# One adaLN block (linear attention and a mixture of experts), with the operations of every engine in a new order

## What is computed

```python
mod = (silu(c) @ wmod).reshape(16, 6, 1, -1)
sa, ca, ga, sb, cb, gb = (mod[:, i] for i in range(6))
ga = (2 * (ga >= 0) - 1) * maximum(abs(ga), 0.25)      # gb likewise
h = layernorm(x) * (1 + ca) + sa
x = x + ga * attn(h)
h = layernorm(x) * (1 + cb) + sb
x = x + gb * ffn(h)

def attn(x):                                           # 16 heads of 8
    q, k, v = x @ Wq.T + bq, x @ Wk.T + bk, x @ Wv.T + bv
    q = softmax(q, over the 8 of a head); k = softmax(k, over tokens)
    out = q @ (k.T @ v)                                # per head
    return layernorm(out) * ln_g + ln_b, then @ Wo.T + bo

def ffn(x):                                            # 8 experts, top 2
    p = softmax(x @ router_w); top_p, top_e = top_k(p, 2)
    return sum over the 2 of top_p * (gelu(x @ w_in[e] + b_in[e]) @ w_out[e] + b_out[e])
```

## Time and profile before

| | |
|---|---|
| median of 3 runs | 365.6 us (364.08 to 366.45) |
| span of the profiled execution | 363.4 us |
| PE busy | 346.1 us (95%) |
| PE weight loads | 305.2 us (84%) |
| DVE busy | 302.1 us (83%) |
| ACT busy | 275.3 us (76%) |
| POOL busy | 224.8 us (62%) |
| chain that ended last | PE 67%, DVE 14%, issue 6%, DMA 5%, ACT 4% |

### The profile page before, as it was taken

How to read it: one execution, slowest core, us unless ns; L and a number is a source line. 1 busy time by engine, 2 the same in 40 slices (tenths; PEclk the granted TensorE clock), 3 DMA queues, 4 the chain that set the end, 5 groups by cost and what they waited for, 6 DMA issues and landing times.

```text
span 363.4 us, 9785 instructions
## 1 busy us (share of the span) xinstructions
PE 346.1 (95%) x3308; PEld 305.2 (84%) x3308; DVE 302.1 (83%) x1068; ACT 275.3 (76%) x500; POOL 224.8 (62%) x219
## 2 busy tenths in 40 slices
PE   8687899999999999989999999999999999999995
PEld 7365679898788989979898988989898989988885
DVE  3989999699799889979799897969998887864733
ACT  4465799877878888788797979797987968696740
POOL 3167454885826568683758758483866778382842
PEclk9878999999999999999999999999999999999999
DMA  7560055531325343170625343340807042244471
GB/s 217 139 236 0 3 178 203 175 120 62 147 87 177 115 164 132 37 249 9 203 92 175 118 170 124 97 169 4 289 3 262 3 150 87 76 190 119 177 262 58
DMA packets 19112, 47.94 MB, mean 132 GB/s; under 512 B 2603, under 2 KB 6390, under 8 KB 18806
## 3 DMA queue, kind: packets, MB, share of 16 engines
q1 hardware_dynamic: 18832, 47.16, 38.1%
q10 hardware_dynamic: 230, 0.15, 0.1%
HBM read 42.82 MB, written 4.48 MB: 130 GB/s over the span
## 4 chain that ended last, share of the span: by engine, by line
PE 67%; DVE 14%; issue 6%; DMA 5%; ACT 4%; POOL 2%; SPq 1%; DVEq 0%; ACTq 0%; POOLq 0%
PE pY L1113 24%; PE pH L1097 7%; PE pH L1098 6%; PE pH L1099 6%; PE pQV L1060 3%; DMA gate_bc<-route_scratch 3%; PE pC L1067 2%; PE pQV L1021 2%; DMA route_scratch<-gateT 2%; PE pC L1054 2%; PE pQV L1037 1%; PE pQV L1023 1%; PE pQV L1022 1%; PE pA L1000 1%; PE pB L1074 1%
## 5 line engine op out<-in xcount | busy, mean ns | idle before, releaser
L1113 PE MATMUL pY<-wout,v 128*128 128x128 f32 x1024 | 129.1, 275 | 0.9 <-DVE v L1630 0.9
L1113 PEld LDWEIGHTS pY<-wout,v 128*128 128x128 f32 x1024 | 124.6, 191 | 5.7 <-DVE v L1630 2.2
L441 POOL TENSOR_TENSOR v<-u,gate_bc 128x512 f32<-128x512 f32 x48 | 68.6, 1433 | 61.3 <-ACT u L769 47.9
L769 ACT ACTIVATE u<-pH,cols 128x512 f32<-128x512 f32 x128 | 85.4, 686 | 15.7 <-PE pH L1099 14.3
L1630 DVE TENSOR_TENSOR v<-u,gate_bc 128x512 f32<-128x512 f32 x80 | 68.0, 858 | 13.3 <-DMA gate_bc<-route_scratch 8.1
L1097 PE MATMUL pH<-h_hi,win_hi 128*128 128x512 f32 x128 | 59.0, 461 | 0.2
L1098 PE MATMUL pH<-h_hi,win_lo 128*128 128x512 f32 x128 | 50.5, 394 | 0.0
L1099 PE MATMUL pH<-h_lo,win_hi 128*128 128x512 f32 x128 | 50.4, 394 | 0.0
L717 ACT ACTIVATE xn<-x_all,nmr,rstd 128x128 f32<-128x128 f32 x64 | 26.3, 485 | 10.3 <-POOL nmr L460 10.2
L453 POOL TENSOR_TENSOR h_lo<-h,h_hi 128x512 fp32r<-128x512 f32 x15 | 20.6, 1370 | 16.1 <-ACT h_hi L697 16.1
L458 POOL TENSOR_TENSOR rstd<-ve,neg_half 128x4 f32<-128x4 f32 x16 | 18.6, 1159 | 18.9 <-DVE nm L1587 18.9
(11 more groups left out here) (169 smaller groups left out, 772.1 us busy)
## 6 DMA issues: line engine op xcount, KB each, us to landing
gate_bc<-route_scratch SPq DMA_DIRECT2D x64, 512.0 KB, 5.1
x_all<-in_L_attn_x SPq DMA_DIRECT2D x16, 256.0 KB, 3.2
out<-x_all SPq DMA_DIRECT2D x15, 256.0 KB, 2.2
gates<-gate_scratch SPq DMA_DIRECT2D x1, 1792.0 KB, 6.2
route_scratch<-gateT SPq DMA_DIRECT2D x64, 4.0 KB
gb_bc<-gb_scratch SPq DMA_DIRECT2D x1, 1024.0 KB, 4.6
win<-in_L_ffn_w_in SPq DMA_DIRECT2D x1, 512.0 KB, 4.3
wout<-in_L_ffn_w_out SPq DMA_DIRECT2D x1, 512.0 KB, 5.6
```

The costliest lines, as they stand in the source:

```text
L441: pool.tensor_tensor(v[:, e % U, :], u[:, e % U, :], gate_bc[:, b % 2, e, :], ALU.mult).then_inc(s["vp_done"], 1)
L769: act.activation(u[:, e % U, :], pH[:, e % 2, :], ACT.Gelu_apprx_tanh, bias=cols[:, e:e + 1]).then_inc(s["gelu_done"], 1)
L1113: i = mm(pY[:, t * P:(t + 1) * P], v[:, e % U, t * P:(t + 1) * P], wout[:, e, :], start=False, stop=(e == NE - 1), skip_group_check=True)
```

## The change

The `step` functions and their loops are gone: all five lists are written out for all 16 batches, in orders that differ from those before from the first calls to the last. The operations themselves are the same. Two helpers get a wait more: `ln1_stats(n)` waits for the aggregates of `ln1_var(n - 1)` and `ln2_stats(n)` for those of `ln2_var(n - 1)`. The diff is some 2,000 lines; this is its core, the beginnings of the lists and the two waits. In the part left out, the lists go on in the same manner to batch 15. At the end of POOL's list `residual2(14)` stands ahead of `weigh(15, 5)`, and the call of `residual2(15)`, which does nothing, is gone.

```diff
--- before.py
+++ after.py
@@ -294,68 +294,114 @@
...
+            load_x(1)
+            load_bias()
             load_experts()
-            load_bias()
-            load_x(1)
             load_x(2)
+            load_x(3)
+            load_x(4)
             store_mod_gates()
-            load_x(3)
+            spread_later_gates()
             spread_first_gates()
+            load_x(5)
             load_expert_bias()
-            spread_later_gates()
-            for b in range(-1, 8):
-                step(b)
+            store_gates(0)
+            spread_gates(0, 0)
+            store_moe_gates()
+            spread_moe_gates()
+            spread_gates(0, 1)
+            load_x(6)
+            spread_gates(0, 2)
+            spread_gates(0, 3)
+            store_gates(1)
+            spread_gates(1, 0)
+            spread_gates(1, 1)
+            load_x(7)
+            spread_gates(1, 2)
+            spread_gates(1, 3)
+            store_gates(2)
+            spread_gates(2, 0)
+            spread_gates(2, 1)
+            store_out(0)
+            spread_gates(2, 2)
+            spread_gates(2, 3)
...
@@ -459,196 +505,173 @@
...
+            masks()
             rstd_L(0)
-            masks()
             rstd_L(1)
+            h_low(1)
             gated_weight(0)
             gated_const(0)
+            gated_const(1)
             rstd_L(2)
-            h_low(1)
-            gated_const(1)
             gated_weight(1)
             rstd_O(0)
             expert_low()
-            rstd_L(3)
             h_low(2)
             rstd_B(0)
             h2_low(0)
+            rstd_L(3)
+            rstd_O(1)
+            rstd_L(4)
             gated_weight(2)
-            rstd_O(1)
-            gated_const(2)
-            h_low(3)
             gated_weight(3)
             rstd_B(1)
             weigh(0, 1)
+            h_low(3)
             weigh(0, 3)
+            weigh(0, 5)
+            gated_const(2)
+            gated_const(3)
+            h2_low(1)
             rstd_O(2)
-            rstd_L(4)
-            h2_low(1)
-            weigh(0, 5)
-            gated_const(3)
+            h_low(4)
...
             rstd_B(15)
+            residual2(12)
             weigh(14, 1)
             weigh(14, 3)
             h2_low(15)
@@ -656,10 +679,8 @@
             residual2(13)
             weigh(15, 1)
             weigh(15, 3)
+            residual2(14)
             weigh(15, 5)
-            residual2(14)
-            for b in range(15, 24):
-                step(b)
...
@@ -768,47 +789,25 @@
...
             ln1_apply(0)
+            h_evac_first()
             attention_weights()
-            h_evac_first()
             exp_k(0)
             ln1_apply(1)
             ek_evac(0)
+            h_evac(1)
             exp_q(0)
             expert_high()
-            h_evac(1)
+            qT_evac(0)
             sw_evac(0)
-            qT_evac(0)
             out_square(0)
+            exp_k(1)
             ln1_apply(2)
-            exp_k(1)
             ek_evac(1)
             h_evac(2)
             exp_q(1)
+            sw_evac(1)
             ln2_apply(0)
-            sw_evac(1)
             qT_evac(1)
             h2_evac(0)
             out_square(1)
@@ -817,114 +816,292 @@
             ln1_apply(3)
             gateT_evac(0)
             ek_evac(2)
-            h_evac(3)
             exp_q(2)
             gelu(0, 0)
+            gelu(0, 1)
+            h_evac(3)
+            gelu(0, 2)
+            gelu(0, 3)
             sw_evac(2)
-            gelu(0, 1)
-            gelu(0, 2)
             qT_evac(2)
-            gelu(0, 3)
+            ln1_apply(4)
+            out_square(2)
             ln2_apply(1)
-            out_square(2)
             gelu(0, 4)
+            gelu(0, 5)
+            gelu(0, 6)
             h2_evac(1)
+            exp_router(1)
             exp_k(3)
-            ln1_apply(4)
+            exp_q(3)
+            gelu(0, 7)
...
@@ -1113,264 +1290,477 @@
...
             modulation()
+            hT_first()
+            turn_rows()
             turn_weights()
-            turn_rows()
-            hT_first()
             residual_gates()
+            kT(0)
             keep_clock()
-            kT(0)
             qv(0)
+            ek_back(0)
             keep_clock()
-            ek_back(0)
+            hT(1)
+            keep_clock()
             gain_centred()
             keep_clock()
-            hT(1)
             state(0)
             keep_clock()
+            kT(1)
+            q_turn(0)
             state_weights(0)
-            keep_clock()
-            q_turn(0)
-            keep_clock()
             attend_centred(0)
-            kT(1)
+            attend_project(0)
             qv(1)
-            attend_project(0)
             ek_back(1)
             hT(2)
+            keep_clock()
             state(1)
+            state_weights(1)
             keep_clock()
             kT(2)
-            state_weights(1)
+            keep_clock()
             q_turn(1)
             h2T(0)
-            keep_clock()
             attend_centred(1)
             logits(0)
             qv(2)
+            hidden(0, 0)
+            ek_back(2)
             keep_clock()
-            ek_back(2)
+            gate_turn(0)
             attend_project(1)
-            gate_turn(0)
             hT(3)
-            hidden(0, 0)
+            state(2)
             hidden(0, 1)
-            state(2)
+            hidden(0, 2)
+            state_weights(2)
+            hidden(0, 3)
+            q_turn(2)
             moe_bias(0)
-            state_weights(2)
-            kT(3)
-            hidden(0, 2)
-            q_turn(2)
-            hidden(0, 3)
             hidden(0, 4)
+            hidden(0, 5)
             attend_centred(2)
             combine(0, 0)
-            h2T(1)
             combine(0, 1)
             qv(3)
-            hidden(0, 5)
+            h2T(1)
+            hidden(0, 6)
+            kT(3)
+            attend_project(2)
+            hidden(0, 7)
             logits(1)
-            attend_project(2)
-            ek_back(3)
-            hidden(0, 6)
             combine(0, 2)
-            hT(4)
             combine(0, 3)
             combine(0, 4)
+            hidden(1, 0)
+            ek_back(3)
             gate_turn(1)
+            hidden(1, 1)
+            hidden(1, 2)
+            combine(0, 5)
+            hT(4)
+            hidden(1, 3)
+            hidden(1, 4)
             state(3)
-            hidden(0, 7)
-            hidden(1, 0)
-            combine(0, 5)
-            hidden(1, 1)
+            combine(0, 6)
+            q_turn(3)
             state_weights(3)
-            combine(0, 6)
-            hidden(1, 2)
-            q_turn(3)
-            hidden(1, 3)
+            kT(4)
+            combine(0, 7)
...
+            attend_centred(6)
+            kT(7)
+            attend_project(6)
+            logits(5)
+            qv(7)
+            ek_back(7)
             hidden(4, 3)
-            h2T(5)
-            kT(7)
-            attend_centred(6)
             hidden(4, 4)
-            logits(5)
+            moe_bias(4)
+            combine(4, 0)
+            combine(4, 1)
+            gate_turn(5)
             hidden(4, 5)
-            qv(7)
-            attend_project(6)
-            moe_bias(4)
             hidden(4, 6)
...
@@ -1466,6 +1856,7 @@
 
             def ln1_stats(n):
                 dve.wait_ge(s[f"x{n % XS}_loaded"], DMA * (n // XS + 1))
+                w(dve, "mv1_done", T * n)
                 for t in range(T):
...
@@ -1574,6 +1965,7 @@
 
             def ln2_stats(n):
                 dve.wait_ge(s["x1_ready"], T * n + T)
+                w(dve, "mv2_done", T * n)
                 for t in range(T):
...
@@ -1650,283 +2042,417 @@
...
             ln1_stats(0)
+            ln1_var(0)
             silu_turned()
-            ln1_var(0)
             ln1_apply_first()
+            ln1_stats(1)
             modulation_columns()
+            h_evac_half()
             columns()
+            h_low_first()
             attention_low()
-            h_evac_half()
-            h_low_first()
+            ln1_var(1)
+            k_max(0)
             attention_gates()
-            k_max(0)
-            ln1_stats(1)
-            ln1_var(1)
+            centring()
             q_bias(0)
-            centring()
             q_max(0)
             q_shift(0)
+            gained_weight()
             v_bias(0)
-            gained_weight()
+            q_sum(0)
+            q_inv(0)
+            q_norm(0)
+            k_inv(0)
+            state_out(0)
+            k_max(1)
             ln1_stats(2)
-            q_sum(0)
-            k_inv(0)
-            q_inv(0)
-            state_out(0)
-            q_norm(0)
             ln1_var(2)
             expert_gates()
+            out_var(0)
             ln1_stats(3)
-            ln1_var(3)
-            out_var(0)
-            k_max(1)
             q_bias(1)
+            v_bias(1)
             q_max(1)
             residual1(0)
-            k_inv(1)
```

(55 more changed lines are left out.)

1280 lines of the change are left out of this document (878 added, 402 removed).

## The result

The change made the kernel 3 to 4% slower. The forecast was 367.6 us, half a per cent slower.

What follows compares the result with a forecast made beforehand. PE was taken as the bound after the fill, with DVE full from 18 to 54 us. Span 363.4 + 0.7 (start) + 1.3 (94 to 340) = 365.4, plus 2.2 to the median: 367.6 us, range 362.0 to 371.5.

Steps and rivals of the forecast that it cites:

- +0.7 us for the start: Lag of finished PE work left at 94 us after the fill; bounds -1.5 to +3.5 us.
- the gb row: Expert gates of batch 0: gb_bc ahead of the second quarter; DVE stands 2.5 us at weigh(0,2), about 0.9 at weigh(0,4).
- +1.3 us for 94 to 340: PE idle from 94 to 340 us: 3.3 us expected against 2.0 before.
- The gates of the first batch: Small broadcast queues behind the large one, gates land at 23.2 us; DVE's sum of squares 1.05 us late.
- the walk: New lists stepped through with trace durations: PE work 2.4 us behind at 60 us, 1.6 at 75, 0.7 at 94.
- Rival 2: Slower by the DMA order: both stalls go through, gaps at upper rate, 372.9 us (370.4 with only the first); chance 0.22.
- my rates: PE idle per us in written-out stretches: 0.0235 early, 0.0035 late, mean 0.0135; 0.9 to 5.8 us from 94 to 340.
- Does a new order make PE's work cheaper?: PE, whole run: 25 fewer switches to three-pass products cost and gain nothing; only idle time can move.
- PE busy changed by more than 1 us: Sign that the forecast is wrong: it would mean neighbours have a price; forecast was within 0.5 us of 346.1.
- the two waits at 0: Added waits in ln1_stats and ln2_stats on DVE: between 0 and 1.1 us over the run, taken as 0.
- the first 12 us: Start: some tenths saved, but first kT at 11.15 us for 10.89, a loss of 0.3 us; ga_rows at about 14.9.
- the drain: End of the last batch: residual2(14) goes ahead of weigh(15,5) while POOL waits anyway; 0 us.

Runs made afterwards that it cites:

- c2_a94: a3_both's orders for what has started by 94 us, the orders of the kernel before behind; 367.39 us, 1.0055 of before.
- a3_both: Changed kernel with the small first-gates broadcast ahead of the large one and the gb row's store and broadcast behind quarters 1 and 2; 370.14 us, 1.0169.
- b1_later: Kernel before with only the 1792 KB broadcast moved ahead of the 256 KB one; 369.51 us, 1.0128 of before.
- f2_again: The changed kernel once more, nothing edited, for a second profile; 380.64 us, 1.0415 of before.
- a1_first: Changed kernel with only the 256 KB broadcast of the first gates issued ahead of the 1792 KB one; 370.34 us, 1.0177 of before.
- c1_waits: Kernel before with its orders written out as lists and the two added waits; 365.25 us, 1.0013 of before.
- h3_both: The same kernel as a3_both, run in another launch on another chip; 370.40 us, 1.0150 of before.
- f1_six: a3_both with six calls on PE's list, where PE idled behind 160 us, moved behind one to three followers; 375.64 us, 1.0281 of before.
- i2_route: i1_mid's kernel with the router chain of batch 6 put back to before's places on all lists; 369.68 us, 1.0137 of before.
- h1_again: The changed kernel again, nothing edited, in a launch on another chip; 379.14 us, 1.0358 of before.
- i1_mid: Kernel before with the changed orders (a3_both's lists) only from 160 to 200 us; 369.78 us, 1.0155 of before.

## Why the prediction was wrong, step by step

Two terms of the sum failed. The +0.7 us for the start stood for 9.5 us by the runs: 6.3 (the first gates), 1.2 (the gb row) and 2.0 (the rest, c2_a94). The +1.3 us for 94 to 340 stood for some 5, and PE's own work, put at 0, was part of that.

**The first gates: the mechanism right, the size wrong three times.** The chain of "The gates of the first batch" came out link by link: `ga_rows` stored at 14.55 (I had it ready at 14.9), the large broadcast issued at 16.01 (16.37 by my sum), the small one behind it at 16.39. Then the first wrong term: from there the 6.2 + 0.6 us were 9.0. The gates were home at 25.0 and not 23.2. I had taken the large broadcast's landing from a trace that issues it at 20.36, not at 16; that it shares the DMA engines with more at 16 is likely, and no run isolates it. The second: from the gates to the sum of squares I allowed 4.1 us and it took 5.1, on a TensorE whose granted clock fell while it stood (0.50 from 24 to 30 us). In a3_both, at a clock of 1.00, the same way takes 4.2 us. The third: without the queue I had the sum of squares at 26.45, and a3_both has it at 24.97. So the queue made it 5.2 us later, and not the 0.85 I priced. `out_var(0)` at 30.22 is 4.0 us behind before's, where I had 1.05, `q_norm(1)` at 39.11 is 3.8 late (forecast 1.2), `hidden(0,0)` starts at 45.42 and not 41.9.

**The lag that was to be worked off.** I had the walk 2.4 us behind at 60 us and 0.7 at 94. Where PE is the bound almost nothing is made up: b1_later, with nothing changed but the swap, is 5.9 us late at the first sum of squares (32.16 against 26.25) and still 5.4 us at the end. Only idle time that the other kernel still has can absorb a lag, and from 54 to 94 us that was the 0.79 us I quoted myself.

**The gb row.** Forecast: the second quarter home at 56.5, DVE standing 2.5 and 0.9 us. Measured: home at 62.0, DVE standing 5.62 and 1.56 (6.46 and 1.64 in f2_again). SP's order was read rightly. But the first quarter was issued at 50.57 and not 47.5, it was 3.9 us and not 2.8 from there to the landing of the 8 KB store, and from there to the landing of the second quarter it was 7.6 us and not 6.2. Rival 2's rule, that it decides if `weigh(0,2)` waits more than about 3 us, was too low a mark: 4.48 us in a1_first cost nothing that could be measured. And on average the other transfer cost far more.

**The gaps from 94 to 340.** I wrote +1.3 us of PE idle. It was +2.5 (4.46 in all against 1.98). That the 4.46 lie inside my 0.9 to 5.8 is luck: my rates took it that a list written out call by call has gaps, and c1_waits, before's orders written out, has none from 160 to 259 us. And the kernel lost about 5 us there, mostly by the orders of 160 to 200, where a wait costs more than its idle time.

**"Does a new order make PE's work cheaper?"** I put 0, and named "PE busy changed by more than 1 us" as what would refute it. It changed by 4.0 us. That new neighbours are the cause is not borne out: a3_both, which has all of them, has 346.1 us, as before has (348.6 in h3_both, the same kernel). What the runs do show is that PE's busy time rises beside each wait and at the lower clock, so a term of 0 for it can't stand beside a term for stalls.

**ACT, which I left out.** I went through the change by engine for the start and by PE's idle rate behind it, and never counted what ACT's order alone brings: six table loads more. The 275.3 of 363.4 us made ACT look idle. The diff shows them outright; what they cost, no run shows.

**Right:** the two waits at 0 (1.0013, 0.9985 to 1.0041), the first 12 us within some tenths (first `kT` at 10.77 where I had 11.15 and before has 10.89, `ga_rows` ready at 14.53 where I had 14.9), the drain (3.64 us against 3.65), and rival 2 as the mechanism, the DMA order. Its 372.9 was still 3 us short. As the sum over parts it should have read: first gates 6.3, gb row 1.2, the rest of the start 2.0 (c2_a94), 160 to 200 some 5. That is 14.5 us, against 13.3 for the mean of 1.0364; the difference is within the errors of the parts. Why the orders of 160 to 200 cost 5 us stays open.

## What to carry to other kernels

- A small transfer that an engine waits for goes ahead of a large one on the same queue; behind it, cost it with a landing measured under the same load. Once TensorE is full, hardly any lag is worked off: what the start loses, the end pays.
- When an order is changed, count what the order itself creates on every engine, such as the activation-table loads at each change between gelu and exp. They are read off the list, and no row of the old trace shows them. Their number is a suspect to test, not yet a price.
- A wait named by the trace is where a delay shows, not always what made it. When engines follow each other in a ring, moving one call, or one chain, can just hand the wait on (f1_six, i2_route). And a wait costs PE more than its idle time: 3.8 us for 2.2 here.

## What the runs showed of the hardware that I had not expected

- 256 KB behind 1792 KB on one queue, issued 0.4 us apart, land 8.6 us after issue against 8.4 for the large one, and 3.4 in before, with no large one ahead. Over the six profiles with the large one first it is 7.5 to 9.2. In a3_both the small one goes first and lands in 4.5, and the large one in 8.5: putting the small first cost the large nothing that shows.
- TensorE's busy time for the same 3308 matmuls ranged from 343.5 us (c2_a94) to 352.4 (a1_first), and to 355.0 in h1_again. A part comes from the first 18 us and differs between executions: 12.03 us in i1_mid and 15.23 in i2_route, which have the same calls there.
- The granted clock from 18 to 54 us was 0.81 in b1_later, where PE stood for the gates. But it is not set by the order alone: a3_both and h3_both are one kernel and had 0.95 and 0.86, and c1_waits, with before's orders, had 0.91 where before had 0.88.
- The changed kernel took 376.0, 380.6 and 379.1 us in three launches in which before took 365.2, 365.2 and 364.8. It differs more between launches than before does; the stall for the second quarter was 5.62, 6.46 and 6.21 us.
